# The first edge pass of a graph network kernel: another order of two exponentials and eight evacuations on ScalarE

## The chip, the cores and the metric

The kernel runs on one core of a Trainium2 chip. The metric is the device time of the whole program in microseconds (us). It was run three times before the change, and once more under the hardware profiler; the trace of that execution is what is read here.

A core has five engines with instruction queues of their own: PE (TensorE, matrix products), DVE (VectorE), ACT (ScalarE), POOL (GpSimd, which here issues the indirect DMAs) and SP (which issues plain DMAs). They meet at semaphores alone. An engine takes its instructions strictly in the order in which the program lists them, so an instruction that waits holds up everything behind it on its engine.

## The reference, cut to what matters

The whole program is a stack of four graph layers, each followed by a mixture-of-experts layer, over 3125 nodes of 256 features and 50,000 edges that are sorted by destination. The change is in the first graph layer alone, a graph attention layer:

```python
h = (x @ W).reshape(n, H, C)                # 8 heads of 32 features
e = a_src[src] + a_dst[dst]                 # a_src, a_dst: h weighed by att_src, att_dst
e = jnp.where(e > 0, e, NEG_SLOPE * e)
m = jax.ops.segment_max(e, dst, num_segments=n)
ex = jnp.exp(e - m[dst])
denom = jax.ops.segment_sum(ex, dst, num_segments=n)
msg = h[src] * (ex / denom[dst])[..., None]
out = jax.ops.segment_sum(msg, dst, num_segments=n).reshape(n, H * C) + bias
```

## The kernel before

The edges lie in tiles of 128 (one edge on each partition), and each tile belongs to one block of 125 destination nodes. There are 416 tiles, taken in 52 groups of eight. The function `gat` makes the maximum, the exponential and the sum in one pass over the edges: it holds a running maximum for each node and head (`most`), and whenever that rises, the sums so far are multiplied by a factor. These are the stages that a group goes through, with the lines of their instructions:

- POOL gathers the eight tiles' rows of 264 numbers, 256 features and 8 scores (L784, `gat_rows`), into one of four buffers. A buffer is free once all eight sums of the group four before are done. POOL also issues four scatters (L333) for another layer in each group.
- DVE makes the one-hot matrices of the destinations (`select`, L799). PE turns them (`turn_one_hots`, L1121). ACT makes the complement (`other_nodes`, L1048), the fp32 copy of the turned ones (`open_one_hots`, L1055), a short copy of the scores (`shorten`, L1042), and the fp32 one-hots (`widen_one_hots`, L1063).
- For the maximum, PE spreads each tile's scores over (node, head) by edge: two products with 512 columns and eight with 128 (`spread_tile`, L1082 and L1085), into two banks of PSUM. ACT evacuates them to bf16 in SBUF (`evacuate`, L1023). Tile t + 2 uses the banks of tile t, so its spreading waits for tile t's evacuation. DVE reduces four tiles at once (`greatest`, L947 and L948, then L956 for each tile), first the early four, then the late four. The room for each half is used anew in each group: the evacuation of the first tile of a half waits until the group before is reduced (`taken`).
- DVE renews the table of the maxima (`raise_tables`, L964, L859, L969). ACT takes the exponential of the rise (`factors`, L1032), with which DVE multiplies the sums so far (L1002).
- PE looks the node's values up for each edge (`look_up`, L1110). DVE makes the scores (`scores`, L978 to L982), ACT takes their exponential (`weigh`, L1036), and DVE scales the rows (`scale`, L988).
- PE sums each tile's rows by node (`sum_of`, L1098) into two further banks in turn, and DVE adds each to the accumulator (`add_up`, L1006). The sum of tile t + 2 waits for the addition of tile t.

The helper `pipeline` writes these out as a software pipeline. In one turn of it each engine goes through its list of stages, in order, and each stage has a lag: a stage of lag 3 works on the group three before the newest. The lists of before are, for DVE, `scores` (lag 3), `greatest` of the late half (2), `raise_tables` (2), `scale` (3), `select` (0), `greatest` of the early half (1), `add_up` of the eight tiles (3); for PE, the eight `spread_tile` (1), `look_up` (2), `turn_one_hots` (0), the eight `sum_of` (3); and for ACT:

```python
pipeline(act, (3, weigh), (1, evacuate(range(H))), (2, factors), (1, evacuate(range(H, G))),
         (0, other_nodes), (0, open_one_hots), (0, shorten), (0, widen_one_hots))
```

G is 8 and H is 4. The functions:

Of the kernel before, what the change touches and what calls it, by code (L numbers as in the profile page):

```python
# [27 lines left out]
G = 8  # L28
# [725 lines left out]
def pipeline(eng, *stages, groups=GROUPS, written_out=False):  # L754

    def step(i, g):
        for lag, stage in stages:
            n = U * i + (g - lag)
            if not isinstance(i, int):
                stage(Group(n, (g - lag) % U, i + (g - lag) // U, 2 * U + g - lag))  # L760
            elif 0 <= n < groups:
                stage(Group(n, n % U, n // U, n))


    for i in range(groups // U if written_out else 2):
        for g in range(U):
            step(i, g)
    if not written_out:
        with eng.Fori(2, groups // U) as i:
            for g in range(U):  # L770
                step(i, g)

    for g in range(max(lag for lag, _ in stages)):
        step(groups // U, g)
# [17 lines left out]
def rows_in(q):  # L792

    return (q.turn + 1) * 16 * G
# [75 lines left out]
def gat(nc, S, A, tables, edges):  # L870
# [5 lines left out]
    H = G // 2  # L876
    bias, ln_w, ln_b = tables.bias, tables.ln_w, tables.ln_b
    node, most, own = tables.node, tables.most, tables.own
    with phase(nc, "gat") as (sb, sem):
# [12 lines left out]
        with nc.Block() as block, ExitStack() as ctx:  # L892
# [15 lines left out]
            @block.sync  # L908
            def _(sp):
                edges.load(sp, 4 * GROUPS + AHEAD)  # L910
                sp.wait_ge(taken, 2 * GROUPS)
                h_rows = S.rows.rearrange("(t p) c -> p t c", p=P)[:, :, 0:D]
                move_rows(sp, own_rows, h_rows[:, 0:NB - 1], own_in)
                move_rows(sp, own_last, h_rows[:, NB - 1], own_in)
                sp.wait_ge(own_in, 2 * ROWS_IN)
# [97 lines left out]
            @block.scalar  # L1013
            def _(act):
                def evacuate(tiles):
                    def stage(q):
                        for t in tiles:
                            half, m = t // H, t % H
                            if m == 0 and q.since(1):
                                act.wait_ge(taken, 2 * q.n - 1 + half)  # L1020
                            act.wait_ge(spread, q.n * G + t + 1)
                            k = 2 * (t % 2)
                            act.copy(wide[half][:, m * HEADS:(m + 1) * HEADS, :],  # L1023
                                     S.ps[0:P, k:k + 2, :].rearrange("p k (h e) -> p (k h) e", e=128))\
                               .then_inc(evacuated, 1)
                    return stage

                def factors(q):
                    act.wait_ge(risen, q.n + 1)
                    if q.since(2):  # L1030
                        act.wait_ge(added, (q.n - 1) * G)
                    act.activation(factor[:, q.slot % 2], rise[:], ACT.Exp).then_inc(factored, 1)  # L1032

                def weigh(q):
                    act.wait_ge(shifted, q.n + 1)
                    act.activation(rows[:, q.slot, :, D:XG], score[:, q.slot % 2], ACT.Exp).then_inc(weighted, 1)  # L1036

                def shorten(q):
                    act.wait_ge(gathered[q.slot], rows_in(q))
                    if q.since(U):  # L1040
                        act.wait_ge(spread, (q.n - U + 1) * G)
                    act.copy(short[:, q.slot], rows[:, q.slot, :, D:XG]).then_inc(rounded, 1)  # L1042

                def other_nodes(q):
                    act.wait_ge(selected, q.n + 1)
                    if q.since(2):
                        act.wait_ge(spread, (q.n - 1) * G)
                    act.activation(other_node[:, q.slot % 2], onehot_b[:, q.slot % 2], ACT.Copy, bias=1.0, scale=-1.0)\  # L1048
                       .then_inc(others, 1)

                def open_one_hots(q):
                    act.wait_ge(turned, q.n + 1)
                    if q.since(2):
                        act.wait_ge(looked_up, q.n - 1)
                    act.copy(onehot_t[:, q.slot % 2],  # L1055
                             S.ps[:, 6, :].bitcast(BF16)[0:P, :].rearrange("p (t e) -> p t e", e=128))\
                       .then_inc(opened, 1)

                def widen_one_hots(q):
                    act.wait_ge(selected, q.n + 1)  # L1060
                    if q.since(U):
                        act.wait_ge(summed, (q.n - U + 1) * G)
                    act.copy(onehot[:, q.slot], onehot_b[:, q.slot % 2]).then_inc(widened, 1)  # L1063

                pipeline(act, (3, weigh), (1, evacuate(range(H))), (2, factors), (1, evacuate(range(H, G))),
                         (0, other_nodes), (0, open_one_hots), (0, shorten), (0, widen_one_hots))

            @block.tensor
# [2305 lines left out]
```

## Time and profile before

| | us |
|---|---|
| runs, lowest / median / highest of 3 | 7785.04 / 7794.26 / 7800.03 |
| the profiled execution, its time | 7782.6 |
| the profiled execution, its span (first to last instruction) | 7780.9 |
| 48 steady groups of this pass, 1250.80 to 2322.70 | 1071.9 |

The span is what the trace covers; the profiled execution's time is 1.7 us more. The profile gives, for each instruction or run of equal ones, its start, its busy time and, in brackets, how long its engine was idle before it and what ended that idleness. PEclk is the clock that TensorE was granted in a stretch, as a share of full speed; there are two levels, 1.2 and 2.4 GHz, so that 0.50 is a stretch at the slow level and 1.00 one at the fast level.

### The profile page before, as it was taken

How to read it: one execution, taken by the hardware profiler on the slowest of the kernel's cores; microseconds unless marked ns; L12 is line 12 of the kernel's file. 1: busy time of each engine (PE TensorE's matmuls, PEld its weight loads, DVE VectorE, ACT ScalarE, POOL GpSimd, SP SyncE). 2: the span in 40 equal slices, each digit the busy share in tenths (PEclk: the TensorE clock that was granted, in tenths of full speed). 3: DMA queues.
4: the chain of work that ended last, by engine and by line, in shares of the span. 5: the costliest groups of instructions: out<-in, count | busy, mean ns of one | idle time of the engine just before them, and what ended most of it. 6: DMA issues, size and time to landing. Idle time of an engine off the chain costs nothing. (4 is left out here: it accounts for less than half of the span.)

```text
span 7780.9 us, 82688 instructions
## 1 busy us (share of the span) xinstructions
PE 4943.0 (64%) x21442; PEld 3404.9 (44%) x21443; DVE 3982.2 (51%) x11544; ACT 2332.1 (30%) x4547; POOL 3440.1 (44%) x3181
## 2 busy tenths in 40 slices
PE   1214966777772886667777467655996555455685
PEld 1103644555552554444554355544664323232474
DVE  8200025777777445677452577784435334343544
ACT  0002334554550112233212355543332222221122
POOL 4773015666662341777203455520003773676043
PEclk6555558988895897888885677777997767776687
DMA  2102432333332434555213222210002332333323
GB/s 46 28 21 69 137 110 80 97 96 95 94 92 65 129 114 62 161 161 164 76 39 86 75 69 71 68 35 14 17 8 70 93 92 60 93 92 92 103 79 103
DMA packets 377709, 633.66 MB, mean 81 GB/s; under 512 B 130352, under 2 KB 258451, under 8 KB 376033
## 3 DMA queue, kind: packets, MB, share of 16 engines
q0 software_dynamic: 146096, 360.51, 16.3%
q1 hardware_dynamic: 231005, 263.55, 12.9%
q10 hardware_dynamic: 308, 6.40, 0.3%
q8 instruction: 91, 1.49, 0.1%
q14 instruction: 209, 1.71, 0.1%
HBM read 474.19 MB, written 155.98 MB: 81 GB/s over the span
## 5 line engine op out<-in xcount | busy, mean ns | idle before, releaser
L784 POOL DMA_INDIRECT conv_rows<-rows_b,index x832 | 849.3, 1021 | 1228.6 <-SPq L2706 882.0
L816 DVE TENSOR_TENSOR acc<-acc,ps 125x257 f32 (+1 forms) x1664 | 701.1, 421 | 923.8 <-DMA acc<-slots,ffn_slot_of 379.8
L2752 PE MATMUL ps<-conv_rows,conv_weight_of 128*125 128x256 f32 x1664 | 624.9, 514 | 605.6 <-issue 269.7
L784 POOL DMA_INDIRECT gat_rows<-rows,index x416 | 558.6, 1343 | 818.8 <-POOLq L93 466.9
L2752 PEld LDWEIGHTS ps<-conv_rows,conv_weight_of 128*125 128x125 f32 x1664 | 359.7, 244 | 870.8 <-issue 538.3
L532 PE MATMUL ps<-front_L_gnn_W_t,front_attr_t 64*125 64x256 f32 x800 | 377.0, 648 | 419.3 <-issue 380.1
L784 POOL DMA_INDIRECT mpnn_rows<-rows_b,index x416 | 478.0, 1149 | 334.2 <-POOLq L1648 151.0
L333 POOL DMA_INDIRECT records_src<-by_src_edge_stage,by_src_edge_slot x400 | 410.1, 1025 | 449.2 <-DMA by_src_edge_stage<-edge_rows 177.9
L784 POOL DMA_INDIRECT hyp_rows<-rows,index x416 | 422.0, 1014 | 399.1 <-PE ps L2359 265.5
L2740 ACT ACTIVATE conv_weight_of<-conv_onehot_b,index 128x125 f32<-128x125 bf16 x832 | 251.5, 386 | 987.5 <-DVE conv_onehot_b L2724 754.4
L499 POOL DMA_INDIRECT records_dst<-front_back,front_dst_addr x400 | 417.4, 1044 | 214.4 <-issue 129.7
L1591 DVE SCALAR_TENSOR_TENSOR room<-ps,ffn_comb,room 125x256 f32<-125x256 f32 x400 | 193.5, 484 | 558.0 <-PE ps L1489 390.3
L532 PEld LDWEIGHTS ps<-front_L_gnn_W_t,front_attr_t 64*125 64x125 f32 x800 | 246.9, 323 | 516.0 <-issue 416.9
L1832 PE MATMUL ps<-mpnn_rows,mpnn_onehot 128*125 128x257 f32 x832 | 316.3, 468 | 210.5 <-ACT mpnn_rows L1789 126.7
L1609 ACT ACTIVATE experts_hid<-ps,experts_consts 128x500 f32<-128x500 f32 (+1 forms) x336 | 230.8, 693 | 726.0 <-PE ps L1451 456.4
L1023 ACT CAST room<-ps 125x1024 bf16<-125x1024 f32 x416 | 405.7, 1011 | 116.9 <-PE ps L1085 47.5
L1489 PE MATMUL ps<-experts_w,experts_hid 128*125 128x256 f32 x1600 | 384.0, 392 | 84.0 <-issue 63.5
L646 DVE TENSOR_TENSOR front_work<-acc,front_att 125x1280 f32<-125x1280 f32 x10 | 14.9, 1492 | 799.1 <-ACT acc L595 798.8
L1082 PE MATMUL ps<-gat_far,gat_other_node 128*125 128x512 bf16 x832 | 276.2, 415 | 223.2 <-ACT room L1023 162.8
L1451 PE MATMUL ps<-room,experts_w 128*128 128x500 f32 (+1 forms) x896 | 364.1, 551 | 52.3 <-DMA experts_w<-in_L_ffn_w 33.2
L1489 PEld LDWEIGHTS ps<-experts_w,experts_hid 128*125 128x125 f32 x1600 | 306.6, 194 | 176.2 <-issue 107.7
L1098 PE MATMUL ps<-gat_rows,gat_onehot 128*125 128x264 f32 x832 | 318.4, 526 | 94.1 <-issue 64.6
(591 smaller groups left out, 10529.6 us busy)
## 6 DMA issues: line engine op xcount, KB each, us to landing
mpnn_edge<-records_src SPq DMA_DIRECT2D x104, 512.0 KB
edge_rows<-front_edge_ring SPq DMA_DIRECT2D x100, 451.5 KB
by_src_edge_stage<-edge_rows SPq DMA_DIRECT2D x100, 451.5 KB
conv_rows<-rows_b,index POOLq DMA_INDIRECT x832
front_attr<-in_edge_attr SPq DMA_DIRECT2D x100, 112.0 KB
rows_b<-acc SPq DMA_DIRECT2D x15, 560.0 KB
second_w<-in_L_ffn_w SPq DMA_DIRECT2D x1, 8192.0 KB
slots<-mlp_y SPq DMA_DIRECT2D x56, 128.0 KB
```

Source lines behind the costliest of these rows:

```text
L333: pool.indirect_dma_start(out=self.S.records["src"], out_offset=bass.IndirectOffsetOnAxis(ap=self.addr[:, c:c + 1], axis=0), in_=self.stag ...
L499: pool.indirect_dma_start(out=S.records["dst"], out_offset=bass.IndirectOffsetOnAxis(ap=dst.addr[0:n, c:c + 1], axis=0), in_=back[:, c, :] ...
L532: ins = pe.matmul(S.ps[0:P, 2 + 2 * (h % 2) + t // 2, (t % 2) * D:(t % 2 + 1) * D], attr_t[:, h % 2, t, :], w1c, start=True, stop=True)
L784: pool.indirect_dma_start(out=rows[:, n % U, t, :], out_offset=None, in_=table, in_offset=bass.IndirectOffsetOnAxis(ap=ends[:, n * G + t:n ...
L816: dve.tensor_tensor(here, here, S.ps[0:P, t % banks, 0:width], ALU.add).then_inc(added, 1)
L1023: act.copy(wide[half][:, m * HEADS:(m + 1) * HEADS, :], S.ps[0:P, k:k + 2, :].rearrange("p k (h e) -> p (k h) e", e=128))\
L1082: pe.matmul(S.ps[0:P, k + j, :], other_node[:, q.slot % 2, t, :], bc_mid(far[:], 4), start=True, stop=False, skip_group_check=True)
L1098: pe.matmul(S.ps[0:P, 4 + t % 2, 0:XG], onehot[:, q.slot, t, :], rows[:, q.slot, t, :], start=True, stop=True).then_inc(summed, 1)
L1451: ins = pe.matmul(S.ps[:, m % BANKS, 0:width], w1[:, h, k, f * 128:(f + 1) * 128], S.xT[:, k, at:at + width], start=k == 0, stop=k == K - 1)
L1489: ins = pe.matmul(S.ps[0:P, 4 + m % 4, 0:D], src[:, j % 2, k, n * P:(n + 1) * P], w2[:, h, k, :], start=k == 0, stop=k == KF - 1)
L1832: pe.matmul(S.ps[0:P, t % 2, 0:D + 1], onehot[:, q.slot % 2, t, :], rows[:, q.slot, t, :], start=True, stop=True).then_inc(summed, 1)
L2752: pe.matmul(S.ps[0:P, t, 0:D], weight_of[:, q.slot, t, :], rows[:, q.slot, t, :], start=True, stop=True).then_inc(summed, 1)
```

## The change

ScalarE's list of stages gets another order. The evacuation of the early four tiles goes ahead of the exponential of the scores, and the evacuation of the late four tiles goes ahead of the factors. No instruction is added or taken away, no buffer changes, and the lists of the other engines stay as they are.

```diff
-                pipeline(act, (3, weigh), (1, evacuate(range(H))), (2, factors), (1, evacuate(range(H, G))),
+                pipeline(act, (1, evacuate(range(H))), (3, weigh), (1, evacuate(range(H, G))), (2, factors),
                          (0, other_nodes), (0, open_one_hots), (0, shorten), (0, widen_one_hots))
```

## Rows read from the trace of the kernel before

**Rows 1.** The steady pass: us, then busy us (instructions) by engine, PEclk, DMA share, GB/s.

```profile
1250.80:2322.70 1071.90, 825.93 (x5764) 602.90 (x5762) 795.83 (x1729) 543.26 (x673) 714.67 (x576) 0.88 0.34 96
```

**Rows 2.** Timeline of VectorE, one group: start us, busy us, instruction, [idle before, releaser].

```profile
1717.40 0.21 DVE L978 TENSOR_TENSOR gat_score<-gat_rows,ps 128x64 f32<-128x64 f32 x1
...
1721.38 0.42 DVE L948 TENSOR_REDUCE gat_red<-room 125x32 f32<-125x256 bf16 x1
...
1724.34 2.28 DVE L988 TENSOR_TENSOR gat_rows<-gat_rows 128x2048 f32<-128x2048 f32 x1
1726.54 1.19 DVE L799 TENSOR_TENSOR gat_onehot_b<-iota,index 128x1000 bf16<-128x1000 f32 x1
1727.65 2.72 DVE L947 TENSOR_TENSOR room<-room 125x2048 bf16<-125x2048 bf16 x4
...
1732.79 0.43 DVE L1002 SCALAR_TENSOR_TENSOR acc<-gat_factor,acc  x1 [0.72 <-issue]
...
1739.16 0.43 DVE L1006 TENSOR_TENSOR acc<-acc,ps 125x264 f32 x1 [0.45 <-PE ps L1098]
1739.50 0.21 DVE L978 TENSOR_TENSOR gat_score<-gat_rows,ps 128x64 f32<-128x64 f32 x1
```

**Rows 3.** Timeline of ScalarE, the same group.

```profile
1718.44 0.26 ACT L1036 ACTIVATE gat_rows<-gat_score 128x64 f32<-128x64 f32 x1 [6.32 <-DVE gat_score L982]
1718.60 1.93 ACT L1023 CAST room<-ps 125x1024 bf16<-125x1024 f32 x2
1720.81 1.93 ACT L1023 CAST room<-ps 125x1024 bf16<-125x1024 f32 x2 [0.28 <-PE ps L1085]
1724.53 0.37 ACT L1032 ACTIVATE gat_factor<-gat_rise 125x200 f32<-125x200 f32 x1 [1.80 <-DVE gat_rise L969]
...
1728.82 1.04 ACT L1048 ACTIVATE gat_other_node<-gat_onehot_b 128x1000 bf16<-128x1000 bf16 x1
...
1732.76 0.24 ACT L1042 CAST gat_short<-gat_rows 128x64 bf16<-128x64 f32 x1 [1.45 <-DMA gat_rows<-rows,index]
```

**Rows 4.** Timeline of TensorE, the same group.

```profile
1717.11 0.62 PE L1085 MATMUL ps<-ident_b,gat_short 128*125 128x128 bf16 x8
...
1719.67 0.65 PE L1082 MATMUL ps<-gat_far,gat_other_node 128*125 128x512 bf16 x2 [1.04 <-ACT room L1023]
...
1725.85 0.65 PE L1082 MATMUL ps<-gat_far,gat_other_node 128*125 128x512 bf16 x2 [1.96 <-ACT room L1023]
...
1727.81 1.95 PE L1110 MATMUL ps<-attention_gat_node,gat_onehot_t 125*128 x16
1729.61 0.66 PE L1121 MATMUL ps<-ident_b,gat_onehot_b 128*125 128x128 bf16 x8
1730.10 1.11 PE L1098 MATMUL ps<-gat_rows,gat_onehot 128*125 128x264 f32 x4
1733.74 5.20 PE L1098 MATMUL ps<-gat_rows,gat_onehot 128*125 128x264 f32 x12 [2.54 <-issue]
```

**Rows 5.** VectorE's timeline where sums come late: first and last of 16 such groups.

```profile
1310.14 0.43 DVE L1002 SCALAR_TENSOR_TENSOR acc<-gat_factor,acc  x1 [0.80 <-issue]
1312.99 1.00 DVE L1006 TENSOR_TENSOR acc<-acc,ps 125x264 f32 x2 [2.42 <-PE ps L1098]
...
2225.76 0.43 DVE L1002 SCALAR_TENSOR_TENSOR acc<-gat_factor,acc  x1 [0.73 <-issue]
2226.50 0.43 DVE L1006 TENSOR_TENSOR acc<-acc,ps 125x264 f32 x1 [0.31 <-PE ps L1098]
```

**Rows 6.** Granted clock by stretch, columns as in rows 1.

```profile
1705.10:1715.30 10.20, 10.20 (x43) 7.78 (x41) 6.19 (x16) 4.40 (x6) 6.83 (x6) 0.52 0.29 92
1718.44:1735.70 17.26, 11.41 (x98) 8.53 (x95) 13.97 (x28) 11.25 (x14) 13.91 (x12) 0.99 0.30 85
1735.80:1739.20 3.40, 3.40 (x9) 2.00 (x9) 1.33 (x4) 0.00 (x0) 0.29 (x1) 0.55 0.35 74
1913.20:1920.10 6.90, 6.52 (x16) 3.80 (x17) 3.20 (x8) 0.21 (x1) 1.94 (x2) 0.52 0.42 126
2034.90:2055.80 20.90, 15.06 (x118) 10.77 (x119) 16.50 (x37) 11.46 (x15) 14.98 (x12) 1.00 0.31 86
1718.44:1740.79 22.35, 16.46 (x124) 11.82 (x121) 16.79 (x37) 11.25 (x14) 15.28 (x13) 0.92 0.33 95
1898.20:1921.40 23.20, 17.40 (x120) 12.58 (x120) 16.66 (x37) 11.43 (x14) 15.06 (x12) 0.85 0.32 92
```

**Rows 7.** TensorE's weight loads at the slow level: the look-up of a group.

```profile
1705.43 3.54 PEld L1110 LDWEIGHTS ps<-attention_gat_node,gat_onehot_t 125*128 125x128 f32 x16
```

## The prediction, as put on record before the result was known

> **What bounds the kernel now.** I cut the view of busy time by stretch to the steady pass and looked at nothing outside it, since the edit touches this pass alone. 48 groups take 1071.9 us, 22.33 us each, and the granted clock averages 0.88 [rows 1]. No engine is busy all of that: VectorE, for one, 795.83 us. So shares decide nothing here, and I read one group's timelines engine by engine.
>
> VectorE's timeline has one unbroken run: from the scores at 1717.40 through the late maxima, the tables, the scaling, the one-hots and the early maxima to the rescaling at 1732.79, 15.4 us, with idle gaps of 0.2 to 0.7 us that are put down to its own issue [rows 2]. Then come eight additions, spaced by the sums that TensorE delivers, the last at 1739.16, and the next scores start 0.34 us later [rows 2]. So a group lasts 15.4 us of VectorE work plus 6.7 us of sums and additions, whatever ScalarE does, as long as three things arrive in time: the exponential for the scaling, the early tiles for the maxima, and the first sums.
>
> ScalarE's timeline shows the two waits that the edit aims at: 6.32 us before the exponential of the scores, and 1.80 us before that of the factors [rows 3]. TensorE pays for both: 1.04 us before tile 2 is spread and 1.96 us before tile 6 [rows 4]. But TensorE then waits 2.54 us before the third sum [rows 4], because that needs the first addition, which is VectorE's. In this group its earlier waits only eat from that slack.
>
> In others they do not. Taking from the rescaling to the first addition, less the 0.47 us that this takes where nothing waits (1732.79 to 1733.26 in the group of rows 2), 16 of the 48 groups have TensorE late, from 2.38 us (1310.14 to 1312.99) to 0.27 us (2225.76 to 2226.50) [rows 5]; the largest is 2.47 and all together are 17.65 us.
>
> The last thing to see is the clock. A group in which TensorE had the fast level throughout takes 20.90 us. The group of rows 2 had it at 0.99 up to 1735.70, then at 0.55 to 1739.20, during its last sums, and takes 22.35. The group from 1898.20 had it at 0.52 during all its sums and takes 23.20 [rows 6]. The slow level does its harm in the sums, and each time TensorE had just done little: short look-up products and a wait of 2 to 2.5 us. It also falls earlier: at 0.52 from 1705.10 to 1715.30 [rows 6] the look-up took 3.54 us where it takes 1.95 [rows 7, 4], and that is how most late groups come about.
>
> **The change part by part.** Nothing is added or removed, so no instruction is priced; only what each waits for changes. I walk the group of rows 2 to 4 again in the new order.
>
> *Early four ahead of the exponential.* Tile 0 is spread by 1717.73 (1717.11 + 0.62) [rows 4], so its evacuation starts near 1717.8 instead of 1718.60, 0.8 us sooner. With a pair of evacuations at 1.93 us [rows 3] and the next pair after 0.28 us, tile 3 is out at 1721.9. The exponential then runs from 1721.9 to 1722.2 instead of at 1718.44: 3.5 us later. Behind it on ScalarE stands the late half; for it waits the scaling, at 1724.34 [rows 2]. That is 2.1 us of cover; price here 0. If the cover went, each us would cost one in each group.
>
> *Late four ahead of the factors.* Tile 4 needs the late half's room, free after the reduction at 1721.38 + 0.42 = 1721.8 [rows 2]: just in time. Its evacuation starts at 1722.2, and two pairs end at 1726.4. The factors wait for nothing by then (what they read was there for their old start at 1724.53 [rows 3]) and end at 1726.8. VectorE uses the factors only in the next turn: 0. TensorE spreads tile 7 by 1725.3 instead of 1727.9, so the 1.96 us wait before tile 6 is gone and the look-up starts 2.5 us sooner.
>
> *What comes sooner, and what does not.* The turning needs the one-hots (1726.54 + 1.19 = 1727.73) [rows 2]: 1727.8 instead of 1729.61. The first two sums follow at 1728.3 instead of 1730.10. ScalarE's complement moves from 1728.82 to 1727.8; the short copy stays at 1732.76, since it waits for the gathered rows [rows 3]. POOL's gathers start when the eighth sum is done, so neither they nor SP's DMAs move within a group. The third sum still waits for the first addition at 1733.26. In this group the gain is 0.
>
> *The late groups.* With the look-up 2.5 us sooner and the turning and first sums 1.8 us sooner, 13 of the 16 late groups (at most 1.91 us late) are on time. In the other three ScalarE stands still for about 4 us in the middle of its evacuations; the exponential may be caught behind that, so they keep some delay. Gain at most 17.65 us; I take 16.
>
> *The clock.* This term has no row in the trace of before, for no group there has TensorE's work laid out like this. In the new order it spreads without a break up to 1725.3, then has a short look-up, a wait for the one-hots, the turning, two sums up to 1729.4, and a wait until 1733.7. Before, the thin stretch began at 1727.8 and its last wait was 2.54 us; now it begins at 1725.3 and the last wait is over 4 us. Rows 6 show the slow level behind such stretches, and 0.52 through all the sums of one group. Bounds: every group all fast, 20.90; every group with slow sums, 23.20 [rows 6]. The level needs thin work ahead of it, and there is now more of it ahead of every group's sums, so I put the all-fast end aside and take the mean group between the partly slow 22.35 and the all-slow 23.20: 22.65, one third of the way, as the level can rise again midway through the sums. This 22.65 holds the late groups' gain already.
>
> The sum, against the profiled execution: 48 x (22.65 - 22.33) = +15.4 us. From it goes 2 us for the three groups with the standstill, which I expect to lose less than before: +13 us. The profiled execution took 7782.6 us and would take 7796. The median of the runs is 11.7 us above it; I forecast against that median, 7794.3 + 13 = 7807 us. Taken apart, the +13 is 16 to 18 us gained on late sums and about 30 lost on slow ones.
>
> A page speaks on this: the Trainium skill, "TensorE: Matmul & The Clock Gate", section "HAM oscillation — how this bites in real kernels", says that a burst of products which follows a long enough wait starts at the slow clock again, and advises packing the work so that there is no such wait. The trace agrees on the direction: 0.55 right after the 2.54 us wait. By that rule the change would lose in the sums what it gains in the spreading; without it the sum would be -16.
>
> **The rivals.**
> *Only the late groups gain* (faster). The slow level covers no more of the sums than now, so the 16 to 17.65 us are kept: 7778. For it: the thin stretch already precedes the sums today, and taking away the 1.96 us wait before tile 6 should keep the look-up at the fast level, which 1705.10 shows it can lack. Against: the last wait before the sums grows. It decides if TensorE's clock over the pass stays at 0.88 or above. If sums became all fast too, it would be 48 x (22.33 - 20.90) = 69 us, 7726; I give that almost nothing.
> *Nothing to be seen.* VectorE's 15.4 us and the sums set the group and the two clock effects cancel: 7794, within 5 us.
> *The exponential comes too late* (slower). If tiles 0 to 3 are spread at the slow level, then at up to twice the spacing: 8 products take 0.62 us at the fast one and one tile 0.9 to 1.1 us, so four take up to 7 us from 1716.7, the exponential ends at 1724.9 and the scaling starts 0.6 us late. In every group, 48 x 0.6 = +29: 7823. For it: the slow level reaches 1739.20, the very start of the next spreading. Against: 2.1 us of cover. It decides once tile 3 is evacuated more than 2.1 us later than in my walk.
> *The largest clock loss.* All sums slow in all groups: 48 x (23.20 - 22.33) = +42, 7836.
>
> **How the numbers follow.** A measurement of this kernel can't tell less than 0.2%, 15.6 us, from no change. My forecast (a net loss of 3 to 30 us) gets 0.55, of which 0.23 lies beyond 15.6; only the late groups gain, 0.15, of which 0.10 beyond; nothing to be seen, 0.15; the late exponential, 0.08; nearly all sums slow, 0.05; sums faster than now, 0.02. Faster 0.12, within 0.2% 0.50, slower 0.38. The forecast's own range is 7797 to 7824. For 8 in 10 I leave 1 in 10 beyond the gain on late groups, 7778, and as much beyond 7830.
>
> **What would show it.** Right: no idle row of 1.8 us before L1032, none of 6 us before L1036 (the wait moves ahead of the first L1023); L988 still 5.9 us or so after the scores' end, with no wait on L1036; L1110 2.5 us sooner against L988; few L1006 rows that wait over 1 us right after L1002; PEclk over the pass below 0.88, with values near 0.5 in the sums; a mean group near 22.65. The prediction is wrong if PEclk over the sums rises, if L988 waits for L1036, or if L1006 shows another releaser than L1098.

## The result, and the profile after

The changed kernel takes 7815.63 us (median of 6 runs, 7806.60 to 7825.13) against 7791.43 us (6 runs) for the kernel before: a ratio of 1.0032, 95% interval 1.0020 to 1.0043. It is 24 us slower. The profiled execution took 7814.41 us, its span 7812.6.

The pass, as in [rows 1]. I let a group run from one start of the scores (L978) to the next; 48 steady groups lie between 1274.60 and 2366.90. Columns: stretch, us, then busy us by engine, clock, DMA share, GB/s.

```profile
1274.60:2366.90 1092.30, 831.39 (x5745) 598.27 (x5743) 795.61 (x1729) 537.85 (x668) 701.45 (x564) 0.86 0.32 92
```

The same 48 groups took 1071.4 us before (1272.00 to 2343.40). So 20.9 us are lost here, 22.76 us a group against 22.32. VectorE is busy as long as before, and TensorE longer, with the same instructions.

One group's timeline of TensorE, to be read against [rows 4]: tiles are spread without the wait of 1.96 us, the look-up comes early, and the wait ahead of the third sum is 4.41 us instead of 2.54. The twelve products behind it take 6.00 us instead of 5.20.

```profile
1757.84 0.65 PE L1082 MATMUL ps<-gat_far,gat_other_node 128*125 128x512 bf16 x2 [0.19 <-ACT room L1023]
...
1759.43 0.65 PE L1082 MATMUL ps<-gat_far,gat_other_node 128*125 128x512 bf16 x2 [0.48 <-ACT room L1023]
...
1760.49 1.95 PE L1110 MATMUL ps<-attention_gat_node,gat_onehot_t 125*128 x16
1762.71 0.68 PE L1121 MATMUL ps<-ident_b,gat_onehot_b 128*125 128x128 bf16 x8 [0.26 <-DVE gat_onehot_b L799]
1763.22 1.11 PE L1098 MATMUL ps<-gat_rows,gat_onehot 128*125 128x264 f32 x4
1768.74 6.00 PE L1098 MATMUL ps<-gat_rows,gat_onehot 128*125 128x264 f32 x12 [4.41 <-issue]
```

VectorE's timeline of that group, as in [rows 2]: the scaling (L988) follows the tables without a wait, so the later exponential is covered; the additions (L1006) come one by one, nearly 1 us apart, where at the fast level they come in pairs every 1.41 us.

```profile
1759.26 2.28 DVE L988 TENSOR_TENSOR gat_rows<-gat_rows 128x2048 f32<-128x2048 f32 x1
1761.46 1.19 DVE L799 TENSOR_TENSOR gat_onehot_b<-iota,index 128x1000 bf16<-128x1000 f32 x1
...
1768.25 1.00 DVE L1006 TENSOR_TENSOR acc<-acc,ps 125x264 f32 x2
1770.19 0.43 DVE L1006 TENSOR_TENSOR acc<-acc,ps 125x264 f32 x1 [0.94 <-DVE acc L1006]
1771.07 0.43 DVE L1006 TENSOR_TENSOR acc<-acc,ps 125x264 f32 x1 [0.45 <-PE ps L1098]
1772.13 0.43 DVE L1006 TENSOR_TENSOR acc<-acc,ps 125x264 f32 x1 [0.63 <-PE ps L1098]
```

The granted clock of that group, as in [rows 6]: the fast level until the first addition, the slow one (0.52) through all the others.

```profile
1752.04:1768.25 16.21, 10.96 (x103) 8.61 (x101) 13.08 (x29) 10.67 (x14) 13.25 (x10) 1.00 0.32 89
1768.30:1775.30 7.00, 6.56 (x17) 3.83 (x17) 3.30 (x8) 0.56 (x1) 2.12 (x3) 0.52 0.38 118
```

Done for all 48 groups of each kernel, these readings give the table that the rest leans on. "Additions" is the stretch from the first addition to the next scores, "ahead" the stretch from the look-up to the first addition; the clock is the mean of the 48 values that the view by stretch gives. "Late" is the waiting for the first sum: the sum over the groups of the time from L1002 to the first L1006, less the 0.47 us that this takes where nothing waits. The group, the additions and both clocks are means over the 48 groups. The look-up is timed from the start of the scores (median).

| kernel | group, us | additions, us | clock in additions | clock ahead | look-up at | late, us |
|---|---|---|---|---|---|---|
| before | 22.32 | 6.01 | 0.785 | 0.855 | 10.70 | 17.6 in 15 groups |
| changed | 22.76 | 6.62 | 0.633 | 0.925 | 8.48 | 8.8 in 3 |

### The profile page after: what moved, and what is told of

The parts are those of the page before. It is cut to its first block and busy times, and to the rows that moved or that the text cites. A ratio compares the mean times of both kernels' runs of the same rounds, so it can differ in the third digit from the quotient of the medians.

```text
span 7812.6 us, 82688 instructions
## 1 busy us (share of the span) xinstructions
PE 4950.4 (63%) x21442; PEld 3411.9 (44%) x21443; DVE 3985.0 (51%) x11544; ACT 2329.1 (30%) x4547; POOL 3450.4 (44%) x3181
## 5 line engine op out<-in xcount | busy, mean ns | idle before, releaser
L1098 PE MATMUL ps<-gat_rows,gat_onehot 128*125 128x264 f32 x832 | 346.4, 574 | 205.0 <-issue 144.4
L2348 PE MATMUL ps<-hyp_nodes,hyp_onehot_t 125*128 x832 | 271.2, 464 | 165.1 <-DVE hyp_X L2253 118.6
```

The source lines that it names most:

```text
L1098: pe.matmul(S.ps[0:P, 4 + t % 2, 0:XG], onehot[:, q.slot, t, :], rows[:, q.slot, t, :], start=True, stop=True).then_inc(summed, 1)
L2348: pe.matmul(S.ps[:, 5 + t % LB, 0:D + 1], onehot_t[:, q.slot % 2, t, :], nodes[:, bass.ds(b, 1), 0:D + 1].rearrange("p a c -> p (a c)"), s ...
```

## The experiments

They ran in three lots, each with runs of the kernel before beside it on the same chip. The kernel before took 7844 us beside the first four, 7835 beside the next four, and 6920 beside the last three, so only ratios are compared from lot to lot. The three lots ran on three different chips, and I call the last one the third chip. In the groups of this pass it hardly differs: the changed kernel takes 22.61 us a group there (e10), and 22.60 in the first comparison without its three late groups. The kernel before has no profile there. Readings of the pass, as in the table above:

| kernel | ratio to before, 95% interval | group, us | additions, us | clock in additions | clock ahead | look-up at | late, us |
|---|---|---|---|---|---|---|---|
| e1 early four ahead only | 1.0002 (0.9991 to 1.0013) | 22.57 | 6.12 | 0.788 | 0.827 | 11.26 | 20.6 |
| e2 factors last only | 1.0002 (0.9989 to 1.0014) | 22.39 | 6.04 | 0.779 | 0.739 | 10.78 | 19.4 |
| e3 changed, filled | 1.0045 (1.0027 to 1.0062) | 23.00 | 6.72 | 0.937 | 0.872 | 8.54 | 13.1 |
| e4 before, filled | 1.0081 (1.0064 to 1.0098) | 23.73 | 7.09 | 0.900 | 0.869 | 10.79 | 33.1 |
| e5 changed, two tiles after the turning | 0.9963 (0.9950 to 0.9977) | 21.64 | 5.57 | 0.991 | 0.710 | 6.72 | 2.7 |
| e6 changed, small fill | 1.0014 (1.0005 to 1.0023) | 22.57 | 6.39 | 0.826 | 0.860 | 8.81 | 8.6 |
| e7 changed, tile 6 held | 1.0092 (1.0077 to 1.0107) | 23.69 | 6.77 | 0.743 | 0.890 | 12.44 | 42.3 |
| e8 before, small fill | 1.0022 (1.0010 to 1.0035) | 22.85 | 6.31 | 0.893 | 0.778 | 11.14 | 27.9 |
| e9 before, two tiles after the turning | 0.9922 (0.9898 to 0.9946) | 21.21 | 5.24 | 0.990 | 0.809 | 6.71 | 0.7 |
| e10 changed, again | 1.0041 (1.0028 to 1.0054) | 22.61 | 6.67 | 0.626 | 0.898 | 7.80 | 0.0 |
| e11 changed, one tile after the turning | 1.0028 (1.0017 to 1.0039) | 22.29 | 6.34 | 0.701 | 0.747 | 6.92 | 0.0 |

**e1 and e2: each half alone.**

The list of before, and the two lists (the rest of the call is left out):

```diff
-(3, weigh), (1, evacuate(range(H))), (2, factors), (1, evacuate(range(H, G))),                    # before
+(1, evacuate(range(H))), (3, weigh), (2, factors), (1, evacuate(range(H, G))),    # e1
+(3, weigh), (1, evacuate(range(H))), (1, evacuate(range(H, G))), (2, factors),    # e2
```

> ScalarE's list has only the first half of the edit: early four tiles, exponential of the scores, factors, late four tiles. Theory of the clock (the change loses because TensorE's thin stretch ahead of the sums begins 2.5 us sooner, and the slow level then covers more of the eight sums): here the factors still hold up tile 6, so the look-up starts when it did before the change; the sums should be about as slow as before. 0 to 12 us over the kernel before, L1110 as far after the scores as before. Rival (the exponential moved behind four evacuations is what costs, by way of the scaling): the whole loss of the change shows here, +20 to +30 us, and L988 waits for L1036.

> Only the second half of the edit: exponential of the scores, early four, late four, factors. Theory of the clock: tile 6 no longer waits for the factors, the look-up starts about 1.7 us sooner than before the change (2.5 in the change), the late groups are gone and the last additions of a group are slower; two thirds of the loss, +8 to +20 us. Rival (the moved exponential): no loss, and the late groups' gain of up to 16 us: -16 to 0 us.

Neither half costs anything that can be measured. In e1 the exponential runs as late as in the change (4.40 us after the scores' start; before it was 1.04) and the scaling starts at 6.93 as ever: the moved exponential is not the cost of the change, and that rival falls. It is not free everywhere, though. In two of e1's 48 groups ScalarE stands still in the early four, the exponential comes out behind that, and the scaling starts 2.57 and 1.14 us late, right at its end; e5 has one such group. e1's group in this profile is 0.25 us longer: 0.11 in the additions, 0.08 by those two groups' scaling, and 0.06 by late first sums, as the look-up is later (TensorE now waits longer before tile 6). But the profiled execution is the slowest of e1's twelve (7860 us, median 7842), and the runs don't confirm a loss. For e2 I had expected an earlier look-up and a loss, and got neither: the look-up starts at 10.78, and the total, 3 us under the kernel before, lies where the rival had put it. TensorE's wait before tile 6 did not vanish, it was spread out, because ScalarE stood idle in the late four although the product that it waits for was done. TensorE's products for tile 5 and then ScalarE's timeline in a group of e2; tile 5's evacuation is the first of the two at 1734.13, 1.87 us after those products ended (1731.64 + 0.62). The trace names a product (L1085) as what ended the wait, and why it lasted that long is open:

```profile
1731.64 0.62 PE L1085 MATMUL ps<-ident_b,gat_short 128*125 128x128 bf16 x8
...
1731.90 1.01 ACT L1023 CAST room<-ps 125x1024 bf16<-125x1024 f32 x1 [0.80 <-PE ps L1085]
1734.13 1.93 ACT L1023 CAST room<-ps 125x1024 bf16<-125x1024 f32 x2 [1.21 <-PE ps L1085]
1736.82 1.01 ACT L1023 CAST room<-ps 125x1024 bf16<-125x1024 f32 x1 [0.77 <-PE ps L1085]
```

So the halves don't add up to the change: only together do they bring the look-up to 8.48, and only then does the loss appear. That fits the theory of the clock, but doesn't prove it.

**e3 and e4: filling TensorE's wait.** Products are added that write an unused part of a PSUM bank and that nobody reads. The edit of e3; e4 has the order of before and smaller numbers, `keep(4)` and `keep(12)`.

```diff
-pipeline(pe, *spreads(0, 1, 2, 3, 4, 5, 6, 7), (2, look_up), (0, turn_one_hots),
-         *sums(0, 1, 2, 3, 4, 5, 6, 7))
+def keep(n):
+    def stage(q):
+        if isinstance(q.n, int) and q.n >= GROUPS - 1:
+            return
+        for _ in range(n):
+            pe.matmul(S.ps[:, 7, 256:512], S.ident_b[:], bc_mid(far[:], 2),
+                      start=True, stop=True, skip_group_check=True)
+    return stage
+
+pipeline(pe, *spreads(0, 1, 2, 3, 4, 5, 6, 7), (2, look_up), (3, keep(6)), (0, turn_one_hots),
+         *sums(0, 1), (3, keep(24)), *sums(2, 3, 4, 5, 6, 7))
```

> The changed order, with products added that nobody reads: in each group from the fourth, 6 of 256 columns after the look-up and 24 of 256 columns between the second and the third sum, about 0.65 and 2.6 us at the fast level, in time in which TensorE waits for VectorE. Theory of the clock: the fast level holds, the eight sums and additions take 6.2 us instead of 6.6 in the mean and no group is late but the three with a standstill: mean group 21.0 to 21.6 us instead of 22.76, 7735 to 7765 us. Rival (the slower sums come from something else than the clock, so more work on TensorE can only hurt): 7815 us or more.

> The order of before, filled in the same way with 4 products of 256 columns after the look-up and 12 between the second and the third sum (0.4 and 1.3 us at the fast level). Theory of the clock: sums fast in most groups, but the wait before tile 6 stays and with it some slow look-ups and late groups: mean group 21.3 to 21.9 us instead of 22.33, 7745 to 7775 us. Rival: 7792 us or more.

Both totals went the other way: 1.0045 and 1.0081. By the totals alone my theory would have fallen. The groups say something else. The clock in the additions rose from 0.633 to 0.937 in e3, and 20 of the 48 groups took under 21.5 us, where the change has 1 and the kernel before 8. Two groups of e3, one at the fast level throughout (first line), and one whose look-up, fill and first sums fell on the slow one (that stretch, then the whole group):

```profile
1828.82:1850.18 21.36, 18.80 (x157) 14.25 (x156) 16.51 (x38) 11.22 (x14) 15.17 (x13) 1.00 0.26 78
1486.00:1499.20 13.20, 12.16 (x68) 10.35 (x69) 7.39 (x14) 6.18 (x8) 9.00 (x7) 0.61 0.25 78
1478.13:1503.80 25.67, 22.75 (x154) 17.69 (x153) 16.52 (x38) 11.23 (x14) 15.08 (x12) 0.80 0.36 103
```

The fill keeps the fast level where it was, but it stands in order ahead of the third sum, and where TensorE comes to it late or slow it is work on the path: 25.67 us. The 20 groups under 21.5 us have the fast level from end to end (1.00); 21 others take over 23.5 us, and each of them has some time at the slow level, somewhere (0.80 to 0.93 over the group).

**e6 and e8: a smaller fill**, `(3, keep(15))` and `(3, keep(8))` between the second and the third sum alone, in the changed kernel (e6) and in the kernel before (e8).

> The changed order with a smaller fill than e3: 15 products of 256 columns that nobody reads, between the second and the third sum only (1.6 us at the fast level, about 3.2 at the slow one, in a wait of 4.3 or 3.4 us, so that it should delay nothing at either level). Theory of the clock: most groups have all sums fast, 21.0 to 21.5 us each; mean group 21.3 to 22.1, 10 to 45 us under the kernel before. Rival (the sums are slow from something else): +20 to +35 us over before.

> The order of before with 8 products of 256 columns that nobody reads between the second and the third sum (0.85 us at the fast level, 1.7 at the slow one, in a wait of 2.5 us). Theory of the clock: more groups with fast sums than the 8 of 48 before, late groups stay (a late group's fill makes it 1.7 us later); mean group 21.9 to 22.6 us, -20 to +12 us. Rival: +0 to +30 us, with sums as slow as before.

Again more groups under 21.5 us (12 and 17) and a higher clock in the additions, and again totals above before and above what the theory had asked for (13 us over before in e6 instead of 10 to 45 under it, 18 over in e8 where 12 was the most), though e6 is within 0.14% of before, better than the change. Late groups grew in e8 to 27.9 us. Three of these four kernels also show idle time of up to 3.5 us before some additions that the trace puts down to nothing in the core: 15.0 us in all before L1006 in e3, 25.1 in e4, 11.9 in e8, none in the kernel before and 4.4 us in e7. Why is open. Padding is no cure here, then, and as a test it is half clean: it shows that the clock answers, and not that the time follows.

**e7: the old wait put back, on TensorE.**

```diff
                         if q.tile_since(t, 2):
                             pe.wait_ge(evacuated, q.n * G + t - 1)
+                        if t == 6 and q.since(2):
+                            pe.wait_ge(scaled, q.n - 1)
```

> The changed order, but TensorE waits before tile 6 until VectorE has scaled the rows (near 1726.6 in the group that the prediction walks through, 0.8 us after tile 6 began in the kernel before): the wait that the change took away is put back, on TensorE alone. Theory of the clock: the thin stretch before the sums is as short as before the change, slow level in the additions back to some 2.8 us of a group from 5.1, and late groups are back; the loss of the change is mostly gone, -5 to +15 us against the kernel before. Rival (the loss comes with ScalarE's order): +20 to +35 us, or more by the late groups.

A miss: 1.0092. The hold was too strong. TensorE waits 3.72 us before tile 6 instead of 1.96, and the slow level follows at once, over the look-up:

```profile
1572.98 0.62 PE L1084 MATMUL ps<-gat_far,gat_other_node 128*125 128x512 bf16 x2 [3.72 <-DVE gat_rows L988]
...
1575.72 3.54 PE L1112 MATMUL ps<-attention_gat_node,gat_onehot_t 125*128 x16
```

30 groups are late, by 42.3 us together. The clock in the additions did rise, from 0.633 to 0.743, most of the way to the 0.785 of before. The run shows the price of a wait in the other place, and not what I built it for.

**e5 and e9: the thin stretch broken up with work that is there anyway.** Tiles 6 and 7 are spread after the turning; e5 has ScalarE's changed order, e9 that of before.

```diff
-pipeline(pe, *spreads(0, 1, 2, 3, 4, 5, 6, 7), (2, look_up), (0, turn_one_hots),
+pipeline(pe, *spreads(0, 1, 2, 3, 4, 5), (2, look_up), (0, turn_one_hots), *spreads(6, 7),
          *sums(0, 1, 2, 3, 4, 5, 6, 7))
```

> The changed order on ScalarE, and on TensorE tiles 6 and 7 are spread after the turning instead of before the look-up; nothing added. TensorE's thin stretch is broken in two: look-up and wait for the one-hots, then 1.8 us of spreading and 1.1 us of sums, then a wait of about 2.5 us before the third sum, as before the change, where the change has over 4. Theory of the clock: slow level in the additions for about 3 us of a group again instead of 5.1, mean group 22.0 to 22.5 us, within 12 us of the kernel before and 10 to 35 us under the change. Rival (the change costs by what ScalarE does, not by TensorE's clock): as the change, +20 to +30 us over before.

> ScalarE's order of before, with e5's order on TensorE (tiles 6 and 7 after the turning). Theory of the clock: e5's gain comes from where TensorE's work lies, and that is nearly the same here, since the factors hold up no tile that the look-up stands behind; -15 to -35 us against the kernel before, slow level in the additions under 1 us of a group. Rival (e5's gain needs the changed order on ScalarE): 0, within 10 us.

This is the clean test. Both expectations named the right side of the rival, and both were too small: e5 was to be within 12 us of the kernel before and is 33 us under it, e9 was to gain 15 to 35 us and gains 47. In e5 nothing is added, ScalarE's order is that of the change, and the group falls from 22.76 to 21.64 us. A group of e5, TensorE's timeline:

```profile
1628.19 1.95 PE L1110 MATMUL ps<-attention_gat_node,gat_onehot_t 125*128 x16 [1.07 <-DVEq L966]
1631.85 0.97 PE L1121 MATMUL ps<-ident_b,gat_onehot_b 128*125 128x128 bf16 x8 [1.71 <-DVE gat_onehot_b L799]
1632.61 1.06 PE L1082 MATMUL ps<-gat_far,gat_other_node 128*125 128x512 bf16 x2
...
1635.77 1.11 PE L1098 MATMUL ps<-gat_rows,gat_onehot 128*125 128x264 f32 x4
1637.81 4.10 PE L1098 MATMUL ps<-gat_rows,gat_onehot 128*125 128x264 f32 x12 [0.93 <-issue]
```

and its clock, ahead of the sums and in the additions:

```profile
1632.70:1636.80 4.10, 4.10 (x26) 2.90 (x24) 2.73 (x9) 1.84 (x2) 3.19 (x4) 0.66 0.26 70
1637.30:1642.40 5.10, 4.33 (x18) 2.39 (x19) 3.27 (x8) 2.85 (x4) 2.27 (x3) 1.00 0.22 78
```

The clock over the whole pass is no higher than in the change, 0.87 against 0.86. What moved is where the slow level falls: ahead of the sums, where VectorE's 15.4 us cover it, and the additions run at 0.991. The twelve products take 4.10 us, not 6.00. The whole kernel is 0.37% faster than before (interval 0.50% to 0.23%). The clock is not all that counts in e5: at the same 0.99 its additions take 5.57 us and those of e9 5.24, and that difference I have not explained.

e9 does the same with ScalarE's old order and is 0.78% faster, 21.21 us a group. So e5's gain does not need the change. In e9, on its chip, ScalarE has no standstill, and the look-up is at 6.71 us (6.72 in e5).

**e10 and e11.**

> The changed kernel as it is, beside e9 and e11 on one chip. If its loss is of the clock and of the schedule alone it should not depend on the chip: +15 to +30 us. If it belonged to one chip's runs: within 10 us of the kernel before.

> The changed order with only tile 7 after the turning. Theory of the clock: half of e5's cure; the wait before the third sum is about 3.4 us (4.3 in the change, 2.5 in e5), so the slow level reaches the additions in some groups: mean group between e5's 21.64 and the change's 22.76, near 22.1, -15 to +10 us against the kernel before. Rival (any interleaving of that kind does it): as e5, -25 to -35 us.

The third chip takes about 900 us less for the kernel as a whole, yet the change loses there too: 1.0041, with 22.61 us a group and 0.626 in the additions. It loses the same way with no late group at all. e11, with one tile after the turning, lies between: 22.29 us and 0.701, so "any interleaving does it" falls; but its total, 1.0028, 20 us over before, lies above the +10 us that I had expected at most. e9, e10 and e11 make a ladder on one chip (e9 with ScalarE's order of before, the other two with the changed one). The 48 groups of each, in that order, columns as above:

```profile
787.80:1805.70 1017.90, 797.58 (x5749) 579.78 (x5746) 794.47 (x1728) 530.64 (x668) 700.10 (x565) 0.91 0.35 99
```

```profile
794.30:1879.50 1085.20, 820.57 (x5749) 590.04 (x5746) 795.28 (x1729) 536.47 (x668) 700.87 (x564) 0.85 0.33 93
```

```profile
796.00:1865.90 1069.90, 873.47 (x5748) 628.74 (x5745) 795.84 (x1728) 531.66 (x668) 699.94 (x564) 0.81 0.33 94
```

The clock over the pass does not order them: e11 has the lowest, 0.81, and is faster than e10 at 0.85. The clock in the additions does: 0.990, 0.701, 0.626 for 21.21, 22.29 and 22.61 us a group. e10's pass is 67 us longer than e9's, and its median 73 us.

## Why the prediction came out right

**What bounds a group** held. From the scores' start to the rescaling VectorE took 15.49 us in the mean (15.47 before), and the sums, with what waiting there was for the first of them, took the rest.

**The early four ahead of the exponential: 0.** Right. The exponential ran 3.4 us later (at 4.40 us after the scores' start, 1.04 before), and the scaling did not move (6.94 and 6.93). In the 48 groups the scaling never waits for it. It does in two of the four groups outside them, by 3.32 us in the very first group, and by 0.32 us in the last, as in the kernel before:

```profile
1237.92 2.29 DVE L988 TENSOR_TENSOR gat_rows<-gat_rows 128x2048 f32<-128x2048 f32 x1 [3.32 <-ACT gat_rows L1036]
```

**The late four ahead of the factors: look-up 2.5 us sooner, no gain in an ordinary group.** It came 2.2 us sooner (8.48 against 10.70). The rest is ScalarE's idling in the late four, 0.58 and 1.17 us in the group shown above, which the walk did not have:

```profile
1758.36 1.01 ACT L1023 CAST room<-ps 125x1024 bf16<-125x1024 f32 x1 [0.58 <-PE ps L1085]
...
1760.55 1.93 ACT L1023 CAST room<-ps 125x1024 bf16<-125x1024 f32 x2 [1.17 <-PE ps L1085]
```

Turning and first sums came 2.1 us sooner, and that was worth nothing, as forecast.

**The late groups: 16 us gained.** Only half: 17.6 us before, 8.8 after. (They were 15 groups, not 16.) The 12 others are on time, as forecast; the three with the standstill are not better. In the prediction they kept "some delay" and brought 2 us. They took 71.1 us before and 75.3 after: one took 24.0 us both times, the other two 2 us more each. This is the term that was mis-sized. In one of these two the clock from 1304.00 to 1315.80 is 0.64, TensorE waits 3.95 us before tile 6, its look-up takes 3.54 us, and the first sum comes 3.2 us late:

```profile
1308.09 1.11 PE L1082 MATMUL ps<-gat_far,gat_other_node 128*125 128x512 bf16 x2 [3.95 <-ACT room L1023]
...
1311.56 3.54 PE L1110 MATMUL ps<-attention_gat_node,gat_onehot_t 125*128 x16
```

```profile
1313.46 0.43 DVE L1002 SCALAR_TENSOR_TENSOR acc<-gat_factor,acc  x1 [0.79 <-issue]
1317.13 0.43 DVE L1006 TENSOR_TENSOR acc<-acc,ps 125x264 f32 x1 [3.23 <-PE ps L1098]
```

What I left out is that a standstill of ScalarE is also a wait of TensorE, with the slow level behind it, in these two groups over the look-up and part of the sums. The third group had its additions at the fast level (1.00) and is late by 2.35 us all the same.

**The clock: the mean group between 22.35 and 23.20, at 22.65.** Right in its mechanism: the long thin stretch came, and the slow level behind it fell on the sums. Without the three late groups the mean is 22.60 (1092.3 less 75.3, over 45), with them 22.76. That it came so near to 22.65 is partly luck, for the third of the way from 22.35 to 23.20 was picked and follows from no row. The additions alone went from 6.01 to 6.62 us, 0.61 x 48 = 29 us; the prediction said about 30. 29 lost less 8.8 gained is 20.5 of the 20.9 us in the 48 groups, where the prediction had 13. The medians differ by 3 us more. The two groups ahead of the 48 take 46.9 us instead of 43.1, and the scaling's wait of 3.32 us, shown above, lies in the first of them; so the late exponential, put at 0, may well have cost that much, once. The medians can't prove it: outside the 48 groups the two profiled executions differ by 10.8 us, more than this.

The chain of cause is shown by more than that one agreement. Within the kernel before, the length of the additions follows the time at the slow level in them: over its 48 groups a straight line gives 5.2 us plus 0.29 for each us at the slow level (twice the missing share of the clock, times the length), with a correlation of 0.97, and over those of the change 5.3 plus 0.28. With the clock itself the length goes at -0.97 and -0.96. The mean time at the slow level in the additions is 2.70 us before and 4.94 after; at 0.28 the 2.24 us more make 0.63, against the 0.61 measured. And the one kernel in which ScalarE keeps the changed order and TensorE's sums get the fast level back (e5) has lost the loss and more.

**The Trainium skill**, "TensorE: Matmul & The Clock Gate", section "HAM oscillation — how this bites in real kernels", says that a long enough wait of TensorE makes the products behind it start at the slow clock. That gave the right sign. But here the stretch ahead of the slow level is not all wait: it holds 1.95 us of look-up with 16-column products, which the trace counts as busy. And the prediction read its row too closely: the 0.55 is not right behind the wait of 2.54 us. The products start at 1733.74 [rows 4], and up to 1735.70 the clock is 0.99 [rows 6]; the slow level came 2 us later. The rows show that it follows such a stretch, and not at what distance.

**The rivals.** "Only the late groups gain": the clock over the pass fell from 0.88 to 0.86, so it did not decide for it. As a sign that was a weak one, for e1 and e2 have 0.85 and 0.86 over the pass without the loss; what tells them from the change is the clock in the additions, 0.788 and 0.779 against 0.633. "The exponential comes too late": excluded for the 48 groups by L988, and as the cause of the loss by e1. "Nothing to be seen": the two clock effects did not cancel. "The largest clock loss": the additions of the mean group are at 0.633 and not near 0.5, and the mean group stays 0.44 us under 23.20.

## What to carry to other kernels

An engine that waits off the critical path can still carry a price: removing TensorE's harmless stops gathered its idleness into one stretch just ahead of its critical work, and that work then ran at the slow clock. Before removing a wait, look in the granted clock by stretch at what TensorE does next; and where it must be thin, lay it out so that real work (here two tiles' spreading) stands between the thin part and the products that others wait for. Padding with products that nobody needs raised the clock but cost more than it gave. In part that is because the padding itself is in order and slow when the clock is; the idle time that came with it is unexplained.

## What was not expected of the hardware

The mean clock of a kernel says little: e5 beats the change by 54 us in 48 groups (22.76 to 21.64 us each) at a clock of 0.87 against 0.86 over the pass. ScalarE shows standstills of 2 to 5 us before its evacuations that no row explains, in all ten kernels profiled in the first comparison and the first two lots, and in none of the three profiled on the third chip. The kernel before took 7791 us in the first comparison, 7844 and 7835 in the next two, and 6920 on the third chip; the change, measured in the first and the last, cost 0.32% and 0.41%.
